# The second attention of a four-layer kernel: who rounds the projections, when the row maxima are taken, and values of two heads projected at once

## The reference

```python
def _L1_attn_ref(x, Wq, bq, Wk, bk, Wv, bv, Wo, bo):
    B, S, D, H, HD = (2, 256, 128, 16, 64)
    q = jnp.einsum('bsd,dhk->bshk', x, Wq) + bq
    k = jnp.einsum('bsd,dhk->bshk', x, Wk) + bk
    v = jnp.einsum('bsd,dhk->bshk', x, Wv) + bv
    depth = q.shape[-1]
    q = q / jnp.sqrt(jnp.asarray(depth, q.dtype))
    attn = jnp.einsum('bqhd,bkhd->bhqk', q, k)
    attn = jax.nn.softmax(attn, axis=-1)
    out = jnp.einsum('bhqk,bkhd->bqhd', attn, v)
    return jnp.einsum('bqhd,hdm->bqm', out, Wo) + bo
...
x = x + _L1_attn_ref(_layernorm(x, axis=-1), L1_attn_Wq, L1_attn_bq, ...)
```

## Time and profile before

| what | value |
|---|---|
| three runs | 3405.69, 3411.26, 3417.11 us; median 3411.26 |
| the profiled execution | 3410.64 us, of which span 3408.8 |
| TensorE busy (matmul) | 3054.8 us, 90% |
| VectorE busy | 2357.4 us, 69% |
| ScalarE busy | 1438.4 us, 42% |
| GpSimd busy | 800.2 us, 23% |
| the stage of this attention | from 979.2 us to about 2562 us |

### The profile page before, as it was taken

The page is one execution under the profiler, slowest core; times in us unless marked ns, Lnnn a source line. Parts: engine busy times, 40 slices in busy tenths (PEclk is TensorE's granted clock), DMA queues, the critical chain, the costliest instruction groups (busy, mean ns, idle before and its releaser), DMA issues. The chain is left out here.

```text
span 3408.8 us, 44140 instructions
## 1 busy us (share of the span) xinstructions
PE 3054.8 (90%) x16200; PEld 1881.8 (55%) x16200; DVE 2357.4 (69%) x4755; ACT 1438.4 (42%) x2539; POOL 800.2 (23%) x621
## 2 busy tenths in 40 slices
PE   5999999999879999999999999999997574666799
PEld 3766666666545555555555555555543242444576
DVE  5788888888247777777777777777735767665553
ACT  3666666666413444444434444444442203001343
POOL 0000000000012444444434444444340000443100
PEclk7999999999778999999999999999998585555798
DMA  3121121110040111111101111111000000000100
GB/s 89 25 47 31 41 48 42 30 43 1 8 112 1 38 38 38 38 38 25 32 19 38 38 38 38 38 25 36 15 1 12 6 2 1 1 1 3 29 1 13
DMA packets 40395, 95.29 MB, mean 28 GB/s; under 512 B 12262, under 2 KB 29340, under 8 KB 30620
## 3 DMA queue, kind: packets, MB, share of 16 engines
q1 hardware_dynamic: 40180, 92.48, 12.2%
HBM read 34.52 MB, written 7.34 MB: 12 GB/s over the span
## 5 line engine op out<-in xcount | busy, mean ns | idle before, releaser
L923 ACT ACTIVATE l1a_PT<-l1a_st 128x512 f32<-128x512 f32 x1024 | 605.7, 598 | 878.5 <-PE l1a_st L832 871.5
L940 DVE TENSOR_REDUCE l1a_m<-l1a_aux 128x1 f32<-128x512 f32 x1024 | 673.4, 686 | 189.2 <-PE l1a_aux L795 173.8
L441 DVE TENSOR_REDUCE l0s_mquad<-l0s_mx 128x1 f32<-128x512 f32 x1024 | 635.5, 684 | 169.5 <-PE l0s_mx L309 169.5
L891 POOL TENSOR_TENSOR l1a_acc<-l1a_acc,l1a_PT 128x1024 f32<-128x1024 f32 x224 | 555.1, 2478 | 717.2 <-ACT l1a_PT L923 717.2
L417 ACT ACTIVATE l0s_PT<-l0s_st 128x512 f32<-128x512 f32 x1024 | 528.7, 602 | 236.8 <-PE l0s_st L325 234.2
L845 PE MATMUL l1a_ov<-l1a_PT,l1a_V 128*64 128x512 f32 x2048 | 512.3, 622 | 0.0
L830 PE MATMUL l1a_st<-l1a_QA,l1a_KA 128*128 128x512 f32 x1024 | 452.1, 442 | 3.2 <-issue 3.1
L325 PE MATMUL l0s_st<-l_QS,l_KS 128*128 128x512 f32 x1024 | 438.1, 431 | 3.7 <-ACT l0s_PT L417 3.6
L309 PE MATMUL l0s_mx<-l_KS,l_QS 120*128 120x512 f32 x1024 | 415.6, 413 | 20.3 <-DMA l_KS<-qk_rows 20.3
L832 PE MATMUL l1a_st<-l1a_QB,l1a_KB 65*128 65x512 f32 x1024 | 414.7, 405 | 0.0
L795 PE MATMUL l1a_aux<-l1a_KA,l1a_QA 128*128 128x512 f32 x1024 | 404.2, 437 | 6.8 <-DMA l1a_QA<-l1a_lo 5.4
(11 more groups left out here) (351 smaller groups left out, 3068.6 us busy)
## 6 DMA issues: line engine op xcount, KB each, us to landing
l1a_KA<-l1a_hi SPq DMA_DIRECT2D x32, 512.0 KB, 8.0
l_QS<-qk_rows SPq DMA_DIRECT2D x64, 192.0 KB
l_KS<-qk_rows SPq DMA_DIRECT2D x64, 192.0 KB
l1a_QA<-l1a_hi SPq DMA_DIRECT2D x16, 512.0 KB, 4.6
l1a_QA<-l1a_lo SPq DMA_DIRECT2D x16, 512.0 KB, 4.1
l1a_QB<-l1a_hi SPq DMA_DIRECT2D x16, 512.0 KB, 4.6
l1a_KB<-l1a_lo SPq DMA_DIRECT2D x16, 512.0 KB, 6.5
qk_rows<-l0s_hi SPq DMA_DIRECT2D x64, 64.0 KB, 6.8
```

The costliest lines, as they stand in the source:

```text
L441: nc.vector.tensor_reduce(mquad[:, u % 2, tile, g:g + 1], mx[:, n % MX0, :], axis=AX.X, op=ALU.max).then_inc(mx_free[n % MX0], 1)
L891: nc.gpsimd.tensor_tensor(acc[:, h % 2, 1, :], first, PT[:, g % PT_SLOTS, :], ALU.add).then_inc(added_pool, 1)
L923: nc.scalar.activation(PT[:, g % PT_SLOTS, (u % 2) * CW:(u % 2 + 1) * CW], st[:, u % ST1, :], ACT.Exp).then_inc(exp_done, 1)
L940: nc.vector.tensor_reduce(m4[:, b, q, c:c + 1], src, axis=AX.X, op=ALU.max).then_inc(aux_read, 1)
```

## The change

Four things in this attention, and nothing outside it:

1. **Rounding.** `full` and its factor are gone. ScalarE writes `hi` straight from the PSUM bank of each qk product (512 columns, bias added by Identity), in steps 16, 18, 20 and 22 behind the step's two exponentials. VectorE then writes `lo` from the same bank as (bank + bias) - `hi` with one operation. GpSimd's subtraction `cut` is gone. The factor 1/8 moved into the exponential (`scale`).
2. **Maxima** are spread over 28 steps instead of 30, and mt stands in step 29 instead of 30.
3. **Values** of two heads are projected by one product: 128 columns of `Wv` per tile of `xnT`, four tasks of four products for each pair of heads, at steps 15 and 17 of both heads of the pair before. `V` holds two pairs.
4. **Semaphores.** Several own-engine waits of VectorE (after `full`, `V`, `sums`, `rinv`, `mrow`, and between the additions to `X`) are gone; others wait on `aux_read` instead.

```diff
-MAX_STEPS = 30
+MAX_STEPS = 28
...
-                if n == MAX_STEPS:
+                if n == MAX_STEPS + 1:
                     out.append(("mt", h + 1, 0))
-                if n in (15, 17):
-                    out.append(("v", h + 1, (n - 15) // 2))
+                if n in (15, 17) and h + 2 < H1 + h % 2:
+                    out.append(("v", h // 2 + 1, 2 * (h % 2) + (n - 15) // 2))
...
-        before = ([("qk", 0, c) for c in range(NC)] + [("v", 0, 0), ("v", 0, 1)] + [("qk", 1, c) for c in range(NC)]
+        before = ([("qk", 0, c) for c in range(NC)] + [("v", 0, c) for c in range(NC)] + [("qk", 1, c) for c in range(NC)]
                   + [("max", 0, i) for i in range(NT * NC)] + [("mt", 0, 0)])
...
-                    sp.wait_ge(hi_done, h + 1)
+                    sp.wait_ge(hi_done, NC * (h + 1))
...
-                        for t in range(8):
-                            last = nc.tensor.matmul(o[:, t * HD1:(t + 1) * HD1], xnT[:, (8 * i + t) * P:(8 * i + t + 1) * P],
-                                                    Wv[:, h, :], start=True, stop=True)
+                        for j in range(TPC):
+                            t = TPC * i + j
+                            last = nc.tensor.matmul(o[:, j * P:(j + 1) * P], xnT[:, t * P:(t + 1) * P],
+                                                    Wv[:, 2 * h:2 * h + 2, :], start=True, stop=True)
...
-                        if kt == 13 and h + 2 < H1:
-                            cut(h + 2)
...
-                def round_hi(h):
-                    act.wait_ge(filled, NC * (h + 1))
-                    if h >= 1:
+                def round_hi(h, i):
+                    act.wait_ge(aux_full, slot[("qk", h, i)] + 1)
+                    if h >= 1 and i == 0:
                         act.wait_ge(placed_a[(h - 1) % 3], 64 * ((h - 1) // 3 + 1))
                         act.wait_ge(placed_b[(h - 1) % 2], 32 * ((h - 1) // 2 + 1))
-                    nc.scalar.activation(hi[:, :], full[:, :], ACT.Copy).then_inc(hi_done, 1)
+                    nc.scalar.activation(hi[:, i * CW:(i + 1) * CW], bank(("qk", h, i)), ACT.Identity,
+                                         bias=bias[:, h:h + 1]).then_inc(hi_done, 1)
...
-                    if n == 24 and h + 2 < H1:
-                        round_hi(h + 2)
+                    if n in (16, 18, 20, 22) and h + 2 < H1:
+                        round_hi(h + 2, (n - 16) // 2)
...
                     elif kind == "qk":
-                        if i == 0 and h >= 1:
-                            dve.wait_ge(lo_done, h)
-                        nc.vector.tensor_scalar(full[:, i * CW:(i + 1) * CW], src, bias[:, h:h + 1], factor[:, :],
-                                                ALU.add, ALU.mult).then_inc(filled, 1)
-                        dve.wait_ge(filled, NC * h + i + 1)
-                        dve.sem_inc(aux_read, 1)
+                        at = slice(i * CW, (i + 1) * CW)
+                        dve.wait_ge(hi_done, NC * h + i + 1)
+                        nc.vector.scalar_tensor_tensor(lo[:, at], src, bias[:, h:h + 1], hi[:, at].bitcast(F32),
+                                                       op0=ALU.add, op1=ALU.subtract).then_inc(aux_read, 1)
```

More of the change, by code:

```diff
@@ L665, in l1_attention @@
         norm(load)
-        full = sb("full", [P, S])
         hi = sb("hi", [P, S], F32R)
@@ L724, in bank, with read @@
             return aux[:, slot[key] % AUX1, :]
+        def read(key):
+            return slot[key] + 1
         ADDS = NT - 1
@@ L741, in place_a @@
                         sp.wait_ge(pv_done, NT * (h - 2))
-                    sp.wait_ge(hi_done, h + 1)
+                    sp.wait_ge(hi_done, NC * (h + 1))
                     for dst, src in ((QA[q, b, :], hi[q, :]), (KA[q, b, :], hi[k, :]), (KA[k, b, :], hi[k, :])):
                         sp.dma_start(dst.bitcast(F32), src.bitcast(F32)).then_inc(placed_a[b], 16)
-                    sp.wait_ge(lo_done, h + 1)
+                    sp.wait_ge(aux_read, read(("qk", h, NC - 1)))
                     sp.dma_start(QA[k, b, :].bitcast(F32), lo[q, :].bitcast(F32)).then_inc(placed_a[b], 16)
@@ L758, in place_maxima @@
                 def place_maxima(h):
-                    sp.wait_ge(m_row, h + 1)
+                    sp.wait_ge(aux_read, read(("mt", h, 0)))
                     sp.dma_start(QB[HD1:HD1 + 1, h % 2, :].rearrange("a (t p) -> a t p", p=P).bitcast(F32),
@@ L786, in aux_task @@
                     elif kind == "sumT":
-                        pe.wait_ge(sums_out, h + 1)
+                        pe.wait_ge(aux_read, read(("sum", h, 0)))
                     elif kind == "out" and i == 0:
@@ L839, in values @@
                     if kt == 0:
-                        pe.wait_ge(v_ready, 2 * (h + 1))
+                        pe.wait_ge(aux_read, read(("v", h // 2, NC - 1)))
                         if h >= 1:
@@ L844, in values @@
                         g = 2 * k + qc // 2
-                        last = nc.tensor.matmul(ov[HD1 * (qc % 2):HD1 * (qc % 2) + HD1, qc // 2, :], V[:, h % 2, kt, :],
+                        last = nc.tensor.matmul(ov[HD1 * (qc % 2):HD1 * (qc % 2) + HD1, qc // 2, :],
+                                                V[:, h // 2 % 2, kt, HD1 * (h % 2):HD1 * (h % 2) + HD1],
                                                 PT[:, g % PT_SLOTS, (qc % 2) * CW:(qc % 2 + 1) * CW],
@@ L871, in _ @@
                 nc.gpsimd.memset(KB[HD1:HD1 + 1, :, :].bitcast(F32), 1.0).then_inc(ones_set, 1)
-                def cut(h):
-                    pool.wait_ge(hi_done, h + 1)
-                    if h >= 1:
-                        pool.wait_ge(placed_a[(h - 1) % 3], 64 * ((h - 1) // 3 + 1))
-                        pool.wait_ge(placed_b[(h - 1) % 2], 32 * ((h - 1) // 2 + 1))
-                    nc.gpsimd.tensor_tensor(lo[:, :], full[:, :], hi[:, :].bitcast(F32), ALU.subtract).then_inc(lo_done, 1)
-                cut(0)
-                cut(1)
                 for h in range(H1):
@@ L887, in _ @@
                         if kt == 1 and h >= 2:
-                            pool.wait_ge(sums_out, h - 1)
+                            pool.wait_ge(aux_read, read(("sum", h - 2, 0)))
                         if kt > 1:
@@ L909, in copy_out @@
                     nc.scalar.activation(osb[:, h % 2, :, :], ov[:, :, :], ACT.Copy).then_inc(o_copied, 1)
-                round_hi(0)
-                round_hi(1)
+                act.wait_ge(w_in, 64)
+                for h in range(2):
+                    for i in range(NC):
+                        round_hi(h, i)
                 for g in range(H1 * STEPS1):
@@ L923, in _ @@
                         nc.scalar.activation(PT[:, g % PT_SLOTS, (u % 2) * CW:(u % 2 + 1) * CW], st[:, u % ST1, :],
[L924 removed]
+                                             ACT.Exp, scale=1.0 / float(np.sqrt(HD1))).then_inc(exp_done, 1)
                     if n == 1 and h >= 1:
                         copy_out(h - 1)
[L927 to L928 removed]
+                    if n in (16, 18, 20, 22) and h + 2 < H1:
+                        round_hi(h + 2, (n - 16) // 2)
                 copy_out(H1 - 1)
@@ L973, in aux_task @@
                                              src.rearrange("p (j q c) -> p q j c", q=NC, c=32)[:, :, :, 0]
-                                             ).then_inc(rinv_done, 1)
-                        dve.wait_ge(rinv_done, h + 1)
-                        dve.sem_inc(aux_read, 1)
-                    else:
+                                             ).then_inc(aux_read, 1)
+                    else:
+                        dve.wait_ge(aux_read, read(("sumT", h, 0)))
+                        if h:
+                            dve.wait_ge(aux_read, read(("out", h - 1, i)))
+                        else:
+                            dve.wait_ge(bo_added, 1)
                         for j in range(TPC):
                             t = TPC * i + j
-                            dve.wait_ge(x_added, 1 + NT * h - (NT - 1 - t) if h else 1)
-                            nc.vector.scalar_tensor_tensor(X[:, t, :], src[:, j * D:(j + 1) * D], rinv[:, b, t:t + 1],
-                                                           X[:, t, :], op0=ALU.mult, op1=ALU.add).then_inc(x_added, 1)
-                        dve.wait_ge(x_added, 1 + NT * h + TPC * (i + 1))
-                        dve.sem_inc(aux_read, 1)
+                            last = nc.vector.scalar_tensor_tensor(X[:, t, :], src[:, j * D:(j + 1) * D], rinv[:, b, t:t + 1],
+                                                                  X[:, t, :], op0=ALU.mult, op1=ALU.add)
+                        last.then_inc(aux_read, 1)
                 def add_rows(g):
```

34 lines of the change are left out of this document (10 added, 24 removed).

## The result

The changed kernel takes **3303.09 us** (median of 4 runs, 3301.53 to 3303.80); the kernel before, run beside it, 3412.92 (3405.69 to 3417.11). The ratio is 0.968, with a 95% interval of 0.9662 to 0.9697: 3.2% faster. The profiled execution took 3303.80 us, its span 3302.0.

The account below looks back on a forecast made before the run. TensorE was taken as the bound inside a head. Stall 41.6, clock 29.3 and values 23.8, less 6.9 at the start, sum to 87.8 us off 3410.64, giving 3323 us; range 3308 to 3353.

Parts of the forecast that it names:

- the values: Values tasks in the loop: 30 old at 1.81 us become 28 new at 1.09 us, gaining 23.8 us.
- the semaphores: VectorE's own waits of 0.2 us each disappear; TensorE waits for none inside a head, so 0 gain.
- What bounds: Inside a head TensorE is the bound, busy 92.6 of 95.6 us; idle time and slow clock can be won.
- The stall: Head end: TensorE's wait ahead of the maxima's transpose, held up through GpSimd's `cut`, vanishes, gaining 41.6 us.
- the clock: Behind each head-end stall TensorE's products run at half clock; without idling those slow stretches go, gaining 29.3 us.
- Rounding: qk tasks: VectorE now waits for ScalarE, bank free 0.7 to 0.8 us later; cost 0, other end 39 us.
- The start: Start of the stage: head 0's maxima begin later, behind head 1's `hi` and `lo`, losing 6.9 us.
- the first: Rival: in 56 qk tasks VectorE waits for ScalarE and TensorE idles, up to 39 us, 3362; chance 0.09.
- the second: Rival: something still idles TensorE at head ends and the clock stays low, 29 us more, 3352; chance 0.06.
- the third: Rival: paired values gain nothing because a product costs by its streamed columns, 24 us more, 3347; chance 0.05.
- the fifth: Rival: at the head end `mneg` is late for another reason, so stall and clock remain, 3394; chance 0.02.
- The fourth: Rival: GpSimd's addition starts before VectorE's at 56 qk tasks and holds it, 134 us more, 3457; chance 0.07.

Follow-up runs that it names:

- e5: e7 plus an unused GpSimd subtraction, reading SBUF twice and writing, where `cut` stood: 3378.35 us, ratio 0.9903.
- e7: Changed kernel with values one head at a time and maxima over 30 steps again, leaving the new rounding and semaphores: 3342.05 us, ratio 0.980.
- e4: Changed kernel with the maxima in 30 steps again and their transpose in step 30: 3315.31 us, ratio 0.9728.
- e3: Kernel before, `cut` kept, with only the maxima in 28 steps and the transpose in step 29: 3389.44 us, ratio 0.9943.
- e1: Changed kernel with the old values tasks, one head at a time in 64-column products: 3333.80 us, ratio 0.9783.
- e10: Changed kernel with 112 unused maxima on VectorE placed behind its addition of exponentials, as control of e9b: 3348.05 us, ratio 0.9824.
- e8: Changed kernel with 8 maxima of head 0 ahead of head 1's four products at the start: 3299.62 us; again on another chip, 3303.70.
- e9b: Changed kernel with two unused maxima ahead of each of VectorE's 56 loop remainders, making its addition later: 3469.48 us, ratio 1.0182.

## Why the prediction was right in kind and 20 us short

The sum was 87.8 us, the span fell by 106.8: 19.0 are missing. The step that failed is the sizing of two terms, the values (put at 23.8 us, measured 29.2) and the semaphores (put at 0, measured 3.1); and the sum had no term for what lies outside the stage (8.2). By the prediction's steps:

- **What bounds.** Right: TensorE, idle only at the head's end. The reading of the page's clock row was worthless, as said above; the windows carried it.
- **The stall, 41.6, and the clock, 29.3.** Right in cause and in size. The half clock of the prediction is the granted one: in the kernel before it is 0.50 behind the wait of 2.93 us (1419.80 to 1425.10) and 1.00 behind that of 0.56 us (2477.00 to 2480.30). `e5` brings both back in part, `e7` and `e4` leave 0.56 us a head and the full clock, the changed kernel nothing. The score products of `e7` and of the kernel before can be matched one by one from each transpose on. Up to the first one behind the next values group the kernel before loses 29.0 us in its 14 heads, against the 29.3 of the sum. What I said of the steps as a cover of their own failed (`e3`): the row's DMA was late instead. It didn't change the sum, because `cut` is gone.
- **Semaphores, 0.** Wrong, 3.1 us; the sum had nothing for them, and only the lower end of the prediction's own range counted with own waits. Between head 1's and head 15's transposes stall and clock give 13 x 2.93 + 0.56 + 29.3 = 68.0; measured are 98.5 - 27.4 (values, `e1`) = 71.1. The missing 3.1 us, 0.2 a head, lie in the middle of the head, where the same matching shows the kernel before lose another 0.22 us in every one of the 14 heads. VectorE and TensorE there, before:

```profile
1561.85 1.13 DVE L981 SCALAR_TENSOR_TENSOR top_X<-l1a_aux,l1a_rinv,top_X 128x128 f32<-128x128 f32 x4 [1.08 <-PE l1a_aux L817]
1563.12 1.89 DVE L940 TENSOR_REDUCE l1a_m<-l1a_aux 128x1 f32<-128x512 f32 x3
```

```profile
1563.95 1.00 PE L795 MATMUL l1a_aux<-l1a_KA,l1a_QA 128*128 128x512 f32 x2
1564.80 0.39 PE L830 MATMUL l1a_st<-l1a_QA,l1a_KA 128*128 128x512 f32 x1
```

and in `e7`, which has the new semaphores:

```profile
1542.09 1.13 DVE L967 SCALAR_TENSOR_TENSOR top_X<-l1a_aux,l1a_rinv,top_X 128x128 f32<-128x128 f32 x4 [1.29 <-PE l1a_aux L816]
1543.13 1.88 DVE L932 TENSOR_REDUCE l1a_m<-l1a_aux 128x1 f32<-128x512 f32 x3
```

```profile
1544.18 0.79 PE L794 MATMUL l1a_aux<-l1a_KA,l1a_QA 128*128 128x512 f32 x2
1544.81 0.40 PE L829 MATMUL l1a_st<-l1a_QA,l1a_KA 128*128 128x512 f32 x1
```

From the start of the four additions to `X` to the maxima behind them VectorE takes 1.27 us before and 1.04 in `e7`. It is about 1.27 in both kernels that keep the own wait there (the kernel before and `e3`) and about 1.04 in the changed kernel, `e1`, `e4`, `e7` and `e10`, which dropped it. The two maximum products of TensorE, which need a bank from VectorE, take 0.85 us start to start before and 0.63 in `e7`. No run changes the waits alone; this is read from the traces.
- **Values, 23.8.** The term that was mis-sized most. Undone, they cost 27.4 + 1.8 = 29.2 us (`e1`). I took 1.09 us for the new task from layer 0; in the loop it is 0.92 or 0.81. The rows of layer 0 were of the same shape, but the product behind the group was another, and start to start holds the handover to that product too. Both groups read 1.16 us as a duration. The cost of the old task, 1.81, was taken in the loop and was right. So 5.4 are missing here; my "a tenth up or down" was too narrow.
- **Rounding at 0.** Right: VectorE waits 0.81 to 1.07 us for `hi` in each of the loop's qk tasks, where I had reckoned with 0.7 to 0.8, and TensorE doesn't wait in any of them. The factor in the exponential costs nothing either: one takes 598 ns before and 599 with the change. But the reason given for it, 23 us of slack a head, isn't the true measure; `e10` lost 41 to 45 us to 1.2 us of load at each of these places.
- **The start, -6.9.** Right: -6.4, through the mechanism described (the maxima start at 1007.34 us where I had 1008.3); `e8` shows that the order of the plan sets it.
- **Head 0.** It gave 9.3 us, of which 2.8 went back at the end of the stage, where the last transpose now comes earlier. Of the 6.5 left, 2.93 are its stall and 1.8 its values; 1.8 had no term. Most of that is the clock at the start of the loop: from the first score product on, the slow products last 6.3 us before and 3.3 in the changed kernel. They last 6.3 us in `e3` too, which has the old start, and 3.3 to 5.0 in the kernels with the new one. So part of it can belong to the change; no run decides that.
- **Outside the stage.** No term. The span of the rest was 6.8 us shorter behind the stage and 1.4 ahead of it. One program, `e8`, has 10.7 us between two executions there, so this can't be told from what executions differ by.

Sum of what was missed: 3.1 + 5.4 + 1.8 + 0.5 at the start + 8.2 outside = 19.0. The 8.5 of the values and the semaphores are the errors of the prediction's own steps; with them right it would have been near 3314, inside its range. That the time still fell 5 us below the range is due to the 8.2 outside and the 1.8 of head 0, which had no term. The changed kernel's second measurement, on another chip, is 3307.34, still 0.7 us below the range.

The rivals: the first and the second did not come, the third is refuted by `e1` (512 columns in all: 1.81 us in eight products, 0.81 or 0.92 in four), the fifth by `e7`. The fourth, at 0.07, was the one to watch. The hold it foresees comes as soon as GpSimd begins first (`e9b`), and its price was put at 2.4 us a place; measured are 2.5 for each held addition. The changed kernel is on the right side of it by 0.36 to 0.61 us (I had reckoned with 0.3), in every head alike.

What stays open: what the semaphores are worth by themselves in a run, what shortens the slow start of head 0, what in the chip holds one of two additions, why a wait of 0.56 us leaves the clock and one of 1.8 us doesn't, and why the clock behind the stage differs between executions.
